# Attention 2: the output scaling one unit sooner, other blocks turned by TensorE, and the factor 255 in the values' scale

## The reference

```python
q = transpose(q * scale, (0, 2, 1, 3)); k = transpose(k, (0, 2, 1, 3)); v = transpose(v, (0, 2, 1, 3))
q = _fq_sym(q, axis=-1)            # rounded to 127 steps, per row
k = _fq_sym(k, axis=-1)
v = _fq_sym(v, axis=2)             # s = max(|v|) / 127 per column, at least 1e-8
attn = einsum('bhqd,bhkd->bhqk', q, k)
attn = softmax(attn, axis=-1)
attn = _fq_unsigned(attn, axis=-1) # s = max / 255; round(x / s) * s
out = einsum('bhqk,bhkd->bhqd', attn, v)
return out.transpose(0, 2, 1, 3).reshape(B, N, C) @ Wp + bp
```

## Time and profile before

| | |
|---|---|
| median of three runs | 895.12 us (892.81, 895.12, 899.02) |
| the profiled execution, its own time | 893.93 us |
| its span in the trace | 892.2 us |
| mean granted clock of TensorE | 0.929 of full |
| busy share of the span: TensorE, VectorE, ScalarE, GpSimd | 84%, 61%, 42%, 41% |
| attention 2, from its first maximum to the transposes of its output | 261.5 to 455.8 us |

### The profile page before, as it was taken

How to read it: one execution, slowest core, us unless ns; L and a number is a source line. 1 busy time by engine, 2 the same in 40 slices (tenths; PEclk the granted TensorE clock), 3 DMA queues, 4 the chain that set the end, 5 groups by cost and what they waited for, 6 DMA issues and landing times.

```text
span 892.2 us, 15038 instructions
## 1 busy us (share of the span) xinstructions
PE 747.1 (84%) x5517; PEld 496.0 (56%) x5517; DVE 547.6 (61%) x1290; ACT 371.8 (42%) x674; POOL 364.2 (41%) x387
## 2 busy tenths in 40 slices
PE   5998899994778878787889799298697769999997
PEld 3444554562635555455555588145255437787776
DVE  3897847337689999999936655395798750000014
ACT  4002023222479989898923133334275313221210
POOL 2941220463047878776700570554032044000124
PEclk9999999997887979988889999699999969999999
DMA  7501127898009999999941375810004125433513
GB/s 239 195 0 48 31 48 213 227 132 72 1 10 175 179 152 185 158 185 161 175 133 48 76 148 119 293 39 8 1 1 186 51 57 170 137 129 109 168 42 119
DMA packets 139730, 103.09 MB, mean 116 GB/s; under 512 B 109857, under 2 KB 124697, under 8 KB 137611
## 3 DMA queue, kind: packets, MB, share of 16 engines
q1 hardware_dynamic: 130756, 79.36, 36.4%
q0 software_dynamic: 7984, 22.16, 12.7%
q10 hardware_dynamic: 918, 0.62, 0.2%
HBM read 65.60 MB, written 11.33 MB: 86 GB/s over the span
## 4 chain that ended last, share of the span: by engine, by line
PE 28%; DVE 12%; issue 9%; POOL 6%; ACT 4%; DMA 3%; POOLq 0%; DVEq 0%; ACTq 0%
PE psum L2414 7%; PE psum L2434 5%; PE psum L1639 3%; PE psum L1654 2%; PE psum L2439 1%; DVE xnT L1427 1%; ACT both L1320 1%; PE psum L132 1%; PE psum L1234 1%; POOL both L573 1%; POOL both L440 1%; POOL both L1789 1%; PE psum L223 1%; DVE both L2233 1%; PE psum L1497 1%
## 5 line engine op out<-in xcount | busy, mean ns | idle before, releaser
L1427 DVE TENSOR_SCALAR_CACHE_REDUCE xnT<-psum,both 128x1024 bf16<-128x1024 f32 x128 | 158.0, 1281 | 16.8 <-PE psum L1234 16.4
L1320 ACT ACTIVATE both<-psum,both 128x1024 f32<-128x1024 f32 x128 | 153.7, 1208 | 15.2 <-DVE xnT L1427 14.8
L1131 POOL TENSOR_SCALAR both<-both 128x1024 f16<-128x1024 f32 x128 | 133.7, 1045 | 48.3 <-ACT both L1320 38.3
L1234 PE MATMUL psum<-both 128*128 128x512 bf16 x256 | 89.1, 436 | 28.2 <-ACT both L1320 25.5
L2511 DVE COPY both<-psum 128x256 f32<-128x256 f32 (+1 forms) x21 | 8.0, 381 | 123.8 <-PE psum L2434 113.4
L1255 PEld LDWEIGHTS psum<-both 128*128 128x128 f16 x1024 | 64.7, 99 | 27.5 <-issue 13.4
L132 PE MATMUL psum<-identb 128*128 128x512 bf16 x217 | 60.1, 421 | 22.9 <-DVE x L970 12.4
L1255 PE MATMUL psum<-both 128*128 128x16 f16 x1024 | 68.8, 172 | 10.8 <-DVE xn L1436 7.3
L573 POOL DMA_INDIRECT both<-moe_y_dram,moe_idx_from x48 | 46.3, 965 | 73.6 <-DMA moe_y_dram<-both 47.1
L2414 PE MATMUL psum<-both 128*128 128x320 f32 x256 | 72.3, 436 | 0.2 <-ACT both L561 0.2
L2475 ACT ACTIVATE both<-psum 128x320 f32<-128x320 f32 x64 | 28.0, 437 | 103.6 <-PE psum L2414 103.6
(11 more groups left out here) (383 smaller groups left out, 1519.2 us busy)
## 6 DMA issues: line engine op xcount, KB each, us to landing
both<-in_l_experts SPq DMA_DIRECT2D x50, 384.0 KB, 4.2
both<-in_l_experts SPq DMA_DIRECT2D x16, 1024.0 KB, 5.5
grouped_y_dram<-both SPq DMA_DIRECT2D x31, 128.0 KB
ctok<-in_ctx SPq DMA_DIRECT2D x2, 1024.0 KB, 7.3
both<-kpad_dram SPq DMA_DIRECT2D x1, 2048.0 KB, 8.1
moe_xn_dram<-xn POOLq DMA_DIRECT2D x4, 512.0 KB, 3.9
moe_y_dram<-both POOLq DMA_DIRECT2D x7, 256.0 KB, 5.2
both<-both SPq DMA_TRANSPOSE x96, 3.4
```

Source lines behind the costliest of these rows:

```text
L1131: nc.gpsimd.tensor_scalar(r2[n % RSLOTS2], e2[:, n % ESLOTS2, :], 255.0, HALF_BASE, ALU.mult, ALU.add).then_inc(sem("r2_ready"), 1)
L1234: last = nc.tensor.matmul(bank[2 * (n % SRING2) + half], qz2[:, h % 2, h // 2, t * P:(t + 1) * P], kT2[:, h // 2, half * 512:(half + 1) * ...
L1320: nc.scalar.activation(e2[:, n % ESLOTS2, :], scores_at(n), ACT.Exp, bias=bias2[:, n:n + 1], scale=s2[:, t * H2 + h:t * H2 + h + 1], accum ...
L1427: nc.vector.tensor_scalar(scaled2[n % 2], scores_at(n), ns2[:, t * H2 + h:t * H2 + h + 1], None, ALU.mult, ALU.min, accum_out=bias2[:, n:n ...
```

## The change

The scaling of a group moves from before maximum n = 40, 72, 104 to before maximum n = 39, 71, 103; the one after the last unit stays. Its first step, the multiplication of the sums by 255, is taken out; `sv2` is divided by 255 once instead, behind its reciprocal. The units that TensorE turns become 2, 6, 10 up to 126, and 127 as well; so 33 in place of 32, and SP issues 95 transposes in place of 96, in another order about the weight loads. `copied_by_vector` follows `turned_by_tensor` by its own rule, so VectorE copies 6, 14 up to 126, and 127. The nine warming matmuls behind the last three values are replaced by four ahead of the turn of 127, into the same bank.

```diff
         def turned_by_tensor(n):
-            return n % 4 == 3
+            return n % 4 == 2 or n == H2 * NT - 1
...
                 if TURN_LAG2 <= n < U + TURN_LAG2 and turned_by_tensor(n - TURN_LAG2):
+                    if n == U + TURN_LAG2 - 1:
+                        awake(4, 4)
                     turn(n - TURN_LAG2)
                 if n >= LAG2:
                     values(n - LAG2)
-                if n >= U + LAG2 - 3:
-                    awake(3, 4)
             awake(4, 0)
...
             seq.step(nc.vector.reciprocal(isv2[:], sv2[:]))
+            seq.mark(nc.vector.tensor_scalar(sv2[:], sv2[:], 1.0 / 255.0, None, ALU.mult))
...
                 some = slice(g * GH2, (g + 1) * GH2)
-                seq.step(nc.vector.tensor_scalar(zs2[:, some, :], zs2[:, some, :], 255.0, None, ALU.mult))
                 seq.step(nc.vector.reciprocal(rz2[:, some, :], zs2[:, some, :]))
...
             for n in range(U):
-                past = n - LAG2 - 1
+                past = n - LAG2
                 if past > 0 and past % (GH2 * NT) == 0:
                     scale_out(past // (GH2 * NT) - 1)
                 top(n)
```

## The result

The changed kernel takes 889.58 us, the median of 10 runs (883.46 to 891.19), beside 896.82 for the kernel before, now also over 10 runs (892.81 to 899.02). The ratio is 0.9911 with a 95% interval of 0.9892 to 0.9930: about 8 us faster, 0.9%. The time forecast was 889.6. That the time came out to within 0.1 us is luck.

The account below looks back on a forecast made before the run. The loop was taken to go at VectorE's pace, idle behind scalings until TensorE brought scores. Scaling 3.6 + factor 1.0 - loads 1.5 + tail 1.2 = 4.3 us; 893.93 - 4.3 = 889.6 us, range 884.0 to 895.5.

Parts of the forecast that it names:

- The scaling sooner: Quantised attention 2 loop: one maximum covers TensorE's values and scores; idle behind three scalings falls from 4.42 to 0.84, 3.6 us gained.
- The formula for what is left: Behind a scaling: TensorE's values and scores time (1.62, 1.18, 1.62 us) less 1.20 us of maximum leaves 0.42, 0, 0.42.
- The factor: Multiplication by 255 leaves the three scalings in the loop, all on VectorE's path: 1.0 us gained.
- The turned blocks and the loads: SP's changed order sends block 8 about 0.65 us late behind each of fifteen weight loads: 1.5 us lost.
- the full price: Cost of one block landing late behind a weight load: 0.85 us.
- The tail: After the last maximum, turns 126 and 127 with four warming matmuls: output transposes sooner, 1.2 us gained at the low clock.
- the case that all goes well: Rival, chance 0.16: TensorE holds its upper clock, no loop idle, tail gives 4.0, loads free: 9.4 us gained, 884.5.
- The load as the end of the gain: Rival, chance 0.12: every block 8 behind fifteen loads lands late, 0.85 us each, 12.8 in all: slower, 900.9 us.
- The wait that only moves: Rival, chance 0.08: turn 34 waits for GpSimd, delaying values 31 and the scaling's multiply; 4.5 us of loop gain gone, 894.1.

Follow-up runs that it names:

- the load in the hole: Changed kernel with each weight load one unit sooner, behind block 5, where block 6 is not sent: ratio 0.9896 to before; with extra warming matmuls too, 0.9881.

## Why the prediction was right, and where its sum was off

*The scaling sooner: right in mechanism, under-sized.* The step was put at 3.6 us, with 0.42 us of idle time left behind two of three scalings at the low clock. The clock stood at 1.00 behind the first scaling of the changed kernel, and no idle time was left behind any. The measured part, together with the factor, is 15.98 - 10.37 = 5.6 us, against 4.6 forecast. The formula for what is left holds: 0.43 us at a clock of 0.50 in the kernel with the scaling sooner alone. What was wrong was to carry the clock of the earlier trace rows over. All profiles together bear this out. In the five executions with the scaling ahead of maximum 40, 72 and 104 the idle piece was 1.18 to 1.27 us in four of fifteen scalings, where the scores took 0.59 to 0.69, and 1.60 to 1.63 in the other eleven, where they took 1.01. In the seven executions with the scaling sooner it was nothing in 17 of 21 and 0.23 to 0.43 in four. So the step gains 1.2 us a scaling at either clock, and the rest of its gain is that the upper clock stood there more often. TensorE waited 2.2 to 3.6 us for the scaling in the old place and 0.6 to 1.7 in the new; that the shorter wait keeps the clock up fits, but is not shown, since in the kernel before the upper clock stood behind the longest of its three waits, 2.65 us.

*The factor: right.* Forecast 1.0 us; in the profiles 1.1 alone and 1.4 in the changed kernel, too little to show in the time. The multiplication took from 0.17 to 0.84 us in the loops of the four kernels that have it; why it varies was not tried.

*The turned blocks and the loads: the load's size agreed, its make-up did not, and a gain was missing.* The sum took 1.5 us lost, two of fifteen blocks at the full price. The load in the middle of the blocks does cost about 1.5, but in many small waits (16 of the values', where there were 4). And against before the loop's rest did not grow: the mean of the four kernels with blocks 3, 7, 11 is 166.7 (167.00, 166.92, 166.67, 166.06), and that of the six with 2, 6, 10 and the load behind 7 is 166.7 too (166.60, 166.77, 167.55, 166.06, 166.13, 167.16). The two with the load in the hole stand at 165.1. So the other blocks bring about as much as the load takes. That they bring anything was not in the sum, and which wait it comes from was not tried. The prediction also read four waits as four late blocks, and block 56 as the exception: in the kernel before, fourteen of the fifteen blocks next behind a load already landed later than the median of all.

*The tail: right in its own size, uncertain in worth.* Forecast 1.2; 1.6 and 1.3 in the two profiles, and 1.3 by the means of the five executions with just this tail (9.75, 10.02, 10.03, 9.73, 10.15) against the three with the old one (11.33, 11.67, 10.68). The low clock that the sum took stood there only in part: 0.50 from 445 to 447 us, 0.97 and 1.00 behind that. That a shorter tail shortens the whole was taken for granted, and for the tail alone it is not shown: the warming alone cut it by 2.4 us and the time by 0.6, with an interval from 2.5 faster to 1.3 slower.

*The rivals.* Of the case that all goes well (9.4 us) the loop came true, by the clock, the tail did not. The load as the end of the gain fell, since its price is about 1.5 us in all and not 12.8. The wait that only moves fell: no idle mark stands ahead of the multiply.

So the sum by measured terms: 5.6 for scaling and factor, nothing for the blocks and loads together, 1.3 to 1.6 for the tail if it counts in full, 7 us of the 8 in the ratio, whose interval reaches from 6.3 to 9.7. The four parts run alone add to 6.6 us by their ratios (4.5, 1.4, 0.6 and 0.1), each with some 2 us to either side.

## What to carry to other kernels

When two engines hand a buffer back and forth, put the emptying ahead of a piece of work whose inputs are already there, so that the other engine's refill runs beside it; moving one instruction by one place was worth more than shortening it. Before a saving that stands ahead of a wait is written off, ask when the waited-for work begins: here it began when the shortened instruction ended, so the wait moved along and the saving counted in full. And a transfer belongs in the issue order where nothing is sent right behind it; a count of the waits for transfers shows where to look, but not the price.

## What the runs showed of the hardware that had not been expected

TensorE's clock decides how much of such an idle piece is left over (nothing at 1.00, 0.43 us at 0.50), and it is not the same in two executions of one program: 0.55 and 1.00 in the same two microseconds of the changed kernel, which is 1.5 us in eight matmuls. Behind a load, blocks come late more evenly than the single late row had let expect. The landing of the transposes in the changed kernel, all 95:

```profile
DMA to landing us min/median/max: 3.1/3.4/5.8
```

The fifteen sent next behind a load took 3.8 to 5.8 us, every one above the median of all; 5.8 is block 56 again. But the fifteen of the kernel before took 3.3 to 6.2, with a median of 4.0 beside 4.1, so the landing hardly changed. What changed is when they are sent: 0.66 to 0.87 us behind the load's own issue in 13 of fifteen, and in 4 of fifteen before. SP's queue about the first load, before and after:

```profile
274.18 0.57 SPq L1579 DMA_DIRECT2D both<-in_l_experts  x1
275.93 10.38 SPq L1155 DMA_TRANSPOSE both<-both  x6
```

```profile
278.09 0.57 SPq L1579 DMA_DIRECT2D both<-in_l_experts  x1
278.75 9.78 SPq L1155 DMA_TRANSPOSE both<-both  x6
```

The Trainium skill, DMA: Bandwidth & Descriptors (Queues, rings and completion order), has a queue's descriptors consumed in ring order on each DMA engine. The fifteen late landings fit this and do not show it: blocks sent behind another block took up to 5.3 us (block 57), and of the four that the kernel before sent at once behind a load two took 5.7 and 6.2, two 3.8 and 4.0.

The price was small all the same: 4.1 us of TensorE's waiting (7.9 against 3.8 with the load in the hole) were worth about 1.5 us of the loop. The wait by itself is a poor measure of it: the values waited 6.0 us for transposes with the factor alone and 3.0 before, and the rest of the loop was 166.06 and 167.00.
